# Latent stage of a small language-model tower: feed-forward up products split 128 + 64 instead of 96 + 96 rows

## The chip, the cores and the metric

One Trainium2 chip, one of its cores, one launch. The metric is the device time of the launch in microseconds. TensorE (PE, with its weight loads shown as PEld), VectorE (DVE), ScalarE (ACT), GpSimd (POOL) and SyncE (SP) each run their own instruction stream and meet at semaphores.

## The reference, cut to what matters

A tower of token embedding, quantised attention, a routed attention, a latent linear-attention block, and a mixture of eight experts, over 32 sequences of 128 tokens with 192 features. The change is in the feed-forward half of the latent block (`_L1_attn_ref`):

```
x = x + attn_out
xn = rmsnorm(x, ffn_ln_w)
ffn_out = jax.nn.silu(xn @ w1) * (xn @ w2) @ w3      # w1, w2: 192 x 512, w3: 512 x 192
return x + ffn_out
```

`xn @ w1` and `xn @ w2` contract over 192 features.

## The kernel before

The stages of the tower run one after the other. The latent stage takes 256 tokens (two tiles of 128) at a time. Two streams `p0` and `p1` alternate, each with four PSUM banks and its own buffers. `in_turns_apart` writes the order out by hand: while one stream does its first part (`..._l_1`: norms, latent attention), the other does its second part (`..._l_2`: projection, residual, feed-forward). A generator's `yield` hands over to the other stream. So one half-iteration is one first part interleaved with one second part, there are 16 pairs of tiles in all, and a loop iteration (`Fori`) holds two half-iterations, with a short DVE step (`chain_over`, L1001) after the second.

Every engine runs its instructions in the order of its program, so that order matters:

- PE in a half-iteration: the latent products of the first part (L951, L958, L1534, L1537); the transposes of the feed-forward input by `turn` (L932, called at L1563); the feed-forward up products by `product` (L958, called at L1566 and L1567, 16 matmuls, which the profile shows as 32 instructions, two to a float32 product); the transposes of the head slots (L1545); the decayed products `products` (L1505, twice 12 matmuls); the feed-forward down product (L1572); `times_v` (L1515); `turned_back` (L1523); `turn` of the attention output.
- ACT: takes the turned feed-forward input (`take_turned`, L943); gates of the first part (L1602 to L1604, L1607 to L1611); exponentials (L1615); the four Silu of the feed-forward (L1641); copies of the slots (L1620).
- DVE: the rotary work (L1401 to L1406), the gates (L1409 to L1417), the head norm (L1422, which waits for POOL), L1424, the padded slots (L1434), then the product of Silu and the second up product (L1478), then L1444.
- POOL: a power over 24 columns for each tile (L1490, twice 4.2 us), and the small powers (L998).

`turn` transposes the 192 features as two chunks of 96: four transposes, output on 96 partitions. `product` adds two matmuls of 96 rows into one bank region. Bank `c` holds columns `c` of both up products, w1's in its first half and w2's in its second, and after both the semaphore `hid_p` is raised, once for each `c`. All weights of this stage and of the one before it are loaded by one SP list (`loads_f + loads_l`) as soon as the attention is done with their place (`s_att`), and the stage before the latent one waits for all of them (`s_wf`).

Of the kernel before, what the change touches and what calls it, by code (L numbers as in the profile page):

```python
# [11 lines left out]
ACT = mybir.ActivationFunctionType  # L12
# [82 lines left out]
def tower(nc, a, out):  # L95

    with ExitStack() as ctx:
# [89 lines left out]
        def halves(name):  # L187
            return AP[name].rearrange("(c p) n -> p c n", c=2)
# [551 lines left out]
        def chunks2(x):  # L740
            return x.rearrange("p (c n) -> p c n", c=2)
# [8 lines left out]
        lw_comp, lw_cat, lw_proj = chunks2(W.take(2 * LAT)), W.take(3 * D + 4 * H + D), chunks2(W.take(2 * D))  # L750
        lw_1, lw_2 = chunks2(W.take(2 * HID)), chunks2(W.take(2 * HID))
        lw_3 = W.take(4 * D).rearrange("p (f n) -> p f n", f=4)
# [30 lines left out]
        def halves_of(name):  # L783
            return AP[name].rearrange("(c p) -> p c", c=2)
# [19 lines left out]
            (lw_cat[:, 3 * D:3 * D + 4 * H], AP["L1_attn_w_reso"]), (lw_cat[:, 3 * D + 4 * H:], AP["L1_attn_w_outgate"]),  # L804
            (lw_proj[0:C], halves("L1_attn_w_proj")), (lw_1[0:C], halves("L1_attn_w1")), (lw_2[0:C], halves("L1_attn_w2")),
            (lw_3, AP["L1_attn_w3"].rearrange("(f p) n -> p f n", f=4)),
            (l_lnw[0:C, :], halves_of("L1_attn_ln_w")), (l_fnw[0:C, :], halves_of("L1_attn_ffn_ln_w")),
            (l_memn[0:C, :], halves_of("L1_attn_memn_w")), (l_hd, rows("L1_attn_head_decay")), (l_temp, rows("L1_attn_temperature")),
            (l_qkn[:, 0:DH], rows("L1_attn_qn_w")), (l_qkn[:, DH:2 * DH], rows("L1_attn_kn_w")),
            (l_rot, AP["rotary"]), (l_cnt, AP["count"]), (l_tri, AP["causal_t"]),  # L810
        ]
        loads_m = [
            (mw_v[0:C], halves("L1_ffn_in_proj_w")[:, :, 2 * D:3 * D]), (mw_o[0:C], halves("L1_ffn_out_proj_w")),
# [122 lines left out]
        def take_turned(a, b, dst, ready, scale=None, bias=None):  # L936

            if scale is None:
                nc.scalar.activation(dst[0:C], chunks2(a.bank[b][0:C, :]), ACT.Copy).then_inc(ready, 1)  # L939
                return  # L940
            for c in range(2):
                kw = {} if bias is None else {"bias": bias[0:C, c:c + 1]}
                ins = nc.scalar.activation(dst[0:C, c, :], a.bank[b][0:C, c * NM:(c + 1) * NM], ACT.Identity,  # L943
                                           scale=scale[0:C, c:c + 1], **kw)
            ins.then_inc(ready, 1)

# [572 lines left out]
        def turned_back(pe, g, a, f, i):  # L1519
# [4 lines left out]
            mm.then_inc(f.out_p, 1)  # L1524

        def tensor_l_1(pe, g, a, f):
            pe.wait_ge(f.xr, per(g, 1, 1))
# [30 lines left out]
        def tensor_l_2(pe, g, a, f):  # L1558
# [3 lines left out]
            pe.wait_ge(f.ffn_in, per(g, 1, 1))  # L1562
            turn(a, a.xr, 2, f.xT_p)  # L1563
            pe.wait_ge(f.xT, per(g, 3, 3))
            for c in range(4):
                product(a, lw_1, slice(c * P, (c + 1) * P), a.bank[c][:, 0:NM])  # L1566
                product(a, lw_2, slice(c * P, (c + 1) * P), a.bank[c][:, NM:2 * NM]).then_inc(f.hid_p, 1)  # L1567
            yield
# [63 lines left out]
        def scalar_l_2(act, g, a, f):  # L1632
            act.wait_ge(f.x, per(g, 1, 1))
            squares(a, a.x, f.squared)
            yield
            act.wait_ge(f.xT_p, per(g, 3, 3))
            take_turned(a, 2, a.xT, f.xT, scale=l_fnw)
            yield
            for c in range(4):
                act.wait_ge(f.hid_p, per(g, 4, c + 1))  # L1640
                nc.scalar.activation(a.sil[:, c, :], a.bank[c][:, 0:NM], ACT.Silu).then_inc(f.silu, 1)  # L1641
# [699 lines left out]
```

## Time and profile before

| | |
|---|---|
| runs | 2418.88, 2419.63, 2421.25 us, median 2419.63 |
| the profiled execution, its own time | 2421.41 us |
| its span | 2419.7 us |
| busy in the span: PE, DVE, ACT, POOL | 69%, 56%, 42%, 21% |
| mean granted TensorE clock | 0.77 of full |

The span is the time from the first to the last instruction; 1.7 us of the profiled execution lie around it. TensorE's granted clock is 1.0 (2.4 GHz) or 0.5 (1.2 GHz); the page's line PEclk gives its mean in tenths for each of 40 slices. The latent stage fills about 918 to 1506 us of the span.

### The profile page before, as it was taken

The page shows a single profiled execution, that of the slowest core. Times are in us where ns is not written, and L with a number is a line of the kernel's source. Part 1 is how long each engine was busy: PE and PEld are TensorE (multiplying, and loading weights), DVE is VectorE, ACT ScalarE, POOL GpSimd, SP SyncE. Part 2 cuts the span into 40 slices and gives each one's busy share as a digit, 9 for nine tenths or more (in the row PEclk, how much of TensorE's full clock was granted, in tenths as well). Part 3 has the DMA queues.
Part 4 walks back from the last instruction along what each step waited for, and adds up shares of the span by engine and source line. Part 5 has one row for each costly group of instructions (what it writes and reads, how often), then busy time and mean ns, then how long its engine had stood idle before and what let it go on. Part 6 is the DMA issues. An engine that isn't in the chain of part 4 may idle for free.

```text
span 2419.7 us, 36535 instructions
## 1 busy us (share of the span) xinstructions
PE 1671.7 (69%) x11952; PEld 1259.0 (52%) x11952; DVE 1349.1 (56%) x4440; ACT 1008.5 (42%) x2807; POOL 496.9 (21%) x376
## 2 busy tenths in 40 slices
PE   0056555476667645777877776688788775999996
PEld 0022111364556534565665665566666663777775
DVE  2967888677677755566555553455555553121221
ACT  0244888673333333445445442233333332444342
POOL 5200111000000003233223221022222222333332
PEclk9975555555787765888888888677877877999998
DMA  3000000002993000000000000000000004777775
GB/s 75 0 0 0 1 0 0 1 0 51 188 191 58 0 1 1 1 0 0 0 0 0 0 0 1 1 21 20 20 20 20 20 20 123 183 177 179 182 176 135
DMA packets 135695, 112.72 MB, mean 47 GB/s; under 512 B 29256, under 2 KB 127784, under 8 KB 135592
## 3 DMA queue, kind: packets, MB, share of 16 engines
q1 hardware_dynamic: 118776, 91.70, 16.1%
q0 software_dynamic: 16864, 20.33, 4.5%
q8 instruction: 29, 0.48, 0.1%
q14 instruction: 26, 0.21, 0.0%
HBM read 69.19 MB, written 45.94 MB: 48 GB/s over the span
## 4 chain that ended last, share of the span: by engine, by line
PE 38%; DVE 21%; issue 18%; ACT 12%; POOL 9%; DVEq 1%; DMA 1%; SPq 0%; POOLq 0%; ACTq 0%
PE bank L2157 6%; PE bank L958 5%; ACT bank L686 5%; PE bank L2142 4%; POOL WK L1490 4%; PE bank L2146 3%; PE bank L1848 2%; POOL WK L998 2%; PE bank L1572 2%; PE bank L951 2%; PE bank L1135 2%; PE bank L932 1%; ACT WK L703 1%; PE bank L536 1%; POOL resid L2286 1%
## 5 line engine op out<-in xcount | busy, mean ns | idle before, releaser
L958 PE MATMUL bank<-WK,R 96*128 96x256 f32 x1088 | 308.2, 444 | 26.6 <-ACT WK L943 15.6
L998 POOL TENSOR_TENSOR WK<-WK,mhalf 128x2 f32<-128x2 f32 (+1 forms) x96 | 81.7, 851 | 1008.3 <-DVE WK L975 585.7
L958 PEld LDWEIGHTS bank<-WK,R 96*128 96x128 f32 x1088 | 237.9, 224 | 75.7 <-ACT WK L943 21.5
L686 ACT ACTIVATE bank<-bank,nbias,sc 128x128 f32<-128x128 f32 x384 | 168.0, 469 | 59.5 <-DVE nbias L379 59.5
L2194 ACT ACTIVATE R<-bank,WK 128x256 f32<-128x256 f32 x234 | 98.2, 471 | 218.2 <-PE bank L2146 218.2
L2049 DVE SCALAR_TENSOR_TENSOR WK<-bank,R,WK 128x192 f32<-128x192 f32 x78 | 29.0, 414 | 266.2 <-PE bank L2157 266.2
L2078 POOL DMA_INDIRECT moe_sum<-WK x78 | 121.5, 1557 | 264.1 <-DVE WK L2049 183.4
L2157 PE MATMUL bank<-R 128*128 128x192 f32 x936 | 169.2, 331 | 0.0
L932 PE MATMUL bank<-ident,WK 128*96 128x128 f32 x384 | 73.6, 324 | 126.0 <-DVE WK L981 82.7
L2157 PEld LDWEIGHTS bank<-R 128*128 128x128 f32 x936 | 150.2, 190 | 13.2 <-issue 13.2
L1490 POOL TENSOR_TENSOR WK<-WK,mhalf 128x24 f32<-128x24 f32 x32 | 133.6, 4190 | 26.1 <-DVE WK L1394 26.1
L583 PE MATMUL bank<-WK 32*128 32x128 bf16 x384 | 58.7, 300 | 108.3 <-DVE WK L372 55.6
L2142 PE MATMUL bank<-R 128*128 128x256 f32 x468 | 126.2, 393 | 1.1 <-ACT R L2185 1.1
L932 PEld LDWEIGHTS bank<-ident,WK 128*96 128x96 f32 x384 | 46.8, 147 | 153.5 <-DVE WK L981 79.8
L943 ACT ACTIVATE WK<-bank,R 96x256 f32<-96x256 f32 x128 | 58.8, 508 | 136.0 <-PE bank L932 135.9
L583 PEld LDWEIGHTS bank<-WK 32*128 32x128 bf16 x384 | 27.5, 118 | 164.7 <-ACT bank L686 102.2
L530 PE MATMUL bank<-identb,WK 128*96 128x128 bf16 x64 | 8.2, 306 | 150.2 <-DVE WK L307 137.9
L951 PE MATMUL bank<-R,WK 96*128 96x192 f32 x384 | 100.3, 419 | 14.1 <-ACT WK L939 11.6
L2142 PEld LDWEIGHTS bank<-R 128*128 128x128 f32 x468 | 84.6, 192 | 20.9 <-issue 13.2
L951 PEld LDWEIGHTS bank<-R,WK 96*128 96x128 f32 x384 | 82.1, 243 | 25.6 <-ACT WK L939 21.1
L1848 PE MATMUL bank<-WK 32*128 32x128 f32 x1536 | 83.7, 366 | 14.3 <-DVE WK L1700 4.5
L1750 DVE RECIPROCAL WK<-bank 128x12 f32<-128x12 f32 x32 | 7.4, 233 | 153.7 <-PE bank L1898 153.2
(476 smaller groups left out, 4032.6 us busy)
## 6 DMA issues: line engine op xcount, KB each, us to landing
moe_rows_in<-zeros SPq DMA_DIRECT2D x1, 25026.0 KB, 137.9
R<-in_L_ffn_w SPq DMA_DIRECT2D x39, 576.0 KB, 4.9
R<-in_L_ffn_w SPq DMA_DIRECT2D x39, 384.0 KB, 3.0
R<-moe_rows_in SPq DMA_DIRECT2D x39, 194.0 KB, 4.7
R<-in_L_ffn_w SPq DMA_DIRECT2D x78, 96.0 KB, 3.7
WK<-in_L_ffn_b SPq DMA_DIRECT2D x39, 96.0 KB, 5.5
moe_sum<-resid POOLq DMA_DIRECT2D x16, 192.0 KB, 2.4
moe_sum<-WK POOLq DMA_INDIRECT x78, 6.0
```

The costliest lines, as they stand in the source:

```text
L583: mm = nc.tensor.matmul(bank[u % 4][:, k * P:(k + 1) * P], qks[32 * j:32 * j + 32, k, i * P:(i + 1) * P], qks[32 * j:32 * j + 32, 3 + k, i ...
L686: ins = nc.scalar.activation(s, s, ACT.Exp, bias=nbias[:, u, k:k + 1], scale=col(SS), accum_out=sums[:, 3 * u + k:3 * u + k + 1])
L932: mm = nc.tensor.transpose(a.bank[b][0:C, c * NM + i * P:c * NM + (i + 1) * P], src[:, i, c * C:(c + 1) * C], ident[:, :])
L951: mm = nc.tensor.matmul(a.bank[b][:, i * D:(i + 1) * D], a.xT[0:C, c, i * P:(i + 1) * P], w[0:C, c, :], start=(c == 0), stop=(c == 1))
L958: mm = nc.tensor.matmul(out, w[0:C, c, m], a.xT[0:C, c, :], start=(c == 0), stop=(c == 1))
L998: nc.gpsimd.tensor_tensor(a.rs[:, 0:n], a.ve[:, 0:n], mhalf[:, 0:n], ALU.pow).then_inc(f.root, 1)
L1490: nc.gpsimd.tensor_tensor(a.rs[:, w], a.ve[:, w], mhalf[:, w], ALU.pow).then_inc(f.root, 1)
L1848: mm = nc.tensor.matmul(a.bank[j][:, k * P:(k + 1) * P], x, y, start=True, stop=True)
L2078: pool.indirect_dma_start(out=acc, out_offset=bass.IndirectOffsetOnAxis(ap=x_id[k % B3][:, t:t + 1].bitcast(U32), axis=0), in_=x_y[k % B3] ...
L2142: nc.tensor.matmul(bank[b + n][:, 0:NR], xw_1a[h][:, q * P:(q + 1) * P], x_T[h][:, 0, :], start=True, stop=False)
L2157: mm = nc.tensor.matmul(bank[4 + t][:, 0:D], x_hid[f][:, t * P:(t + 1) * P], xw_2[h][:, f, :], start=(p == 0 and n == 0), stop=(p == PAIRS ...
L2194: ins = nc.scalar.activation(x_hid[q], bank[(0, 2, 0)[p] + n][:, 0:NR], ACT.Gelu, bias=xb_1[h][:, q:q + 1])
```

## The change

The feature axis of the feed-forward input is split into its first 128 features and a rest of 64. `turn_doubled` transposes the first 128 and brings the rest to partitions 0 to 63 and again to 64 to 127, each by a matmul with the identity. `hidden` computes the hidden chunks in pairs: for each of w1 and w2 two matmuls over 128 rows, then two over 64 rows, the first with rows 0 to 63 into one bank, the second with rows 64 to 127 into the other. The rest rows of the weights are loaded so that the odd chunks lie on the upper partitions. `hid_p` is raised once for each pair of chunks.

```
-        lw_1, lw_2 = chunks2(W.take(2 * HID)), chunks2(W.take(2 * HID))
+        lw_1a, lw_2a, lw_1b, lw_2b = W.take(HID), W.take(HID), W.take(HID // 2), W.take(HID // 2)
...
-            (lw_proj[0:C], halves("L1_attn_w_proj")), (lw_1[0:C], halves("L1_attn_w1")), (lw_2[0:C], halves("L1_attn_w2")),
+            (lw_proj[0:C], halves("L1_attn_w_proj")), (lw_1a, AP["L1_attn_w1"][0:P, :]), (lw_2a, AP["L1_attn_w2"][0:P, :]),
...
-            (l_lnw[0:C, :], halves_of("L1_attn_ln_w")), (l_fnw[0:C, :], halves_of("L1_attn_ffn_ln_w")),
+            (l_lnw[0:C, :], halves_of("L1_attn_ln_w")), (l_fnw[:, 0:1], column("L1_attn_ffn_ln_w", 0, P)),
+            (l_fnw[0:HE, 1:2], column("L1_attn_ffn_ln_w", P, HE)), (l_fnw[HE:P, 1:2], column("L1_attn_ffn_ln_w", P, HE)),
...
+        for dst, name in ((lw_1b, "L1_attn_w1"), (lw_2b, "L1_attn_w2")):
+            for n in range(2):
+                loads_l.append((dst[HE * n:HE * (n + 1), :].rearrange("p (f n) -> p f n", f=2),
+                                AP[name][P:D, :].rearrange("p (f two n) -> p f two n", two=2, n=P)[:, :, n, :]))
...
+        def turn_doubled(a, src, b, ready):
+
+            for i in range(M):
+                w = slice(NM + i * P, NM + (i + 1) * P)
+                nc.tensor.transpose(a.bank[b][:, i * P:(i + 1) * P], src[:, i, 0:P], ident[:, :])
+                for n in range(2):
+                    mm = nc.tensor.matmul(a.bank[b][HE * n:HE * (n + 1), w], src[:, i, P:D], ident[:, :], start=True, stop=True)
+            mm.then_inc(ready, 1)
+
+        def take_doubled(a, b, dst, ready, scale):
+
+            for c in range(2):
+                ins = nc.scalar.activation(dst[:, c, :], a.bank[b][:, c * NM:(c + 1) * NM], ACT.Identity, scale=scale[:, c:c + 1])
             ins.then_inc(ready, 1)
...
+        def hidden(a, f, p):
+
+            for wa, wb, out in ((lw_1a, lw_1b, slice(0, NM)), (lw_2a, lw_2b, slice(NM, 2 * NM))):
+                for n in range(2):
+                    c = 2 * p + n
+                    nc.tensor.matmul(a.bank[c][:, out], wa[:, c * P:(c + 1) * P], a.xT[:, 0, :], start=True, stop=False)
+                for n in range(2):
+                    s = slice(HE * n, HE * (n + 1))
+                    mm = nc.tensor.matmul(a.bank[2 * p + n][:, out], wb[s, p * P:(p + 1) * P], a.xT[s, 1, :], start=False,
+                                          stop=True)
+            mm.then_inc(f.hid_p, 1)
...
-            turn(a, a.xr, 2, f.xT_p)
+            turn_doubled(a, a.xr, 2, f.xT_p)
             pe.wait_ge(f.xT, per(g, 3, 3))
-            for c in range(4):
-                product(a, lw_1, slice(c * P, (c + 1) * P), a.bank[c][:, 0:NM])
-                product(a, lw_2, slice(c * P, (c + 1) * P), a.bank[c][:, NM:2 * NM]).then_inc(f.hid_p, 1)
+            hidden(a, f, 0)
+            hidden(a, f, 1)
...
-            take_turned(a, 2, a.xT, f.xT, scale=l_fnw)
+            take_doubled(a, 2, a.xT, f.xT, l_fnw)
...
-                act.wait_ge(f.hid_p, per(g, 4, c + 1))
+                act.wait_ge(f.hid_p, per(g, 2, c // 2 + 1))
```

## Rows read from the trace of the kernel before

**Rows 1.** The page: the span, and the granted clock in 40 slices, in tenths.

```profile
span 2419.7 us, 36535 instructions
...
PEclk9975555555787765888888888677877877999998
```

**Rows 2.** Timeline of POOL, its power L1490: start, us, operation, idle before.

```profile
959.90 8.62 POOL L1490 TENSOR_TENSOR WK<-WK,mhalf 128x24 f32<-128x24 f32 x2 [1.76 <-DVE WK L1394]
...
1171.88 8.31 POOL L1490 TENSOR_TENSOR WK<-WK,mhalf 128x24 f32<-128x24 f32 x2 [1.76 <-DVE WK L1394]
1206.21 8.35 POOL L1490 TENSOR_TENSOR WK<-WK,mhalf 128x24 f32<-128x24 f32 x2 [0.70 <-DVE WK L1394]
1243.46 8.31 POOL L1490 TENSOR_TENSOR WK<-WK,mhalf 128x24 f32<-128x24 f32 x2 [1.76 <-DVE WK L1394]
...
1421.18 8.36 POOL L1490 TENSOR_TENSOR WK<-WK,mhalf 128x24 f32<-128x24 f32 x2 [0.70 <-DVE WK L1394]
```

**Rows 3.** Timeline of a half-iteration whose turn falls at the full clock.

```profile
1206.64 0.64 PE L932 MATMUL bank<-ident,WK 128*96 128x128 f32 x4 [0.29 <-DVE WK L1472]
1208.20 7.17 PE L958 MATMUL bank<-WK,R 96*128 96x256 f32 x32 [0.92 <-ACT WK L943]
1214.60 0.56 DVE L1422 TENSOR_TENSOR WK<-WK 128x384 f32<-128x384 f32 x1 [2.47 <-POOL WK L1490]
1216.97 1.53 PE L1545 MATMUL bank<-ident,WK 128*128 128x128 f32 x12 [1.59 <-DVE WK L1434]
1217.42 1.21 ACT L1641 ACTIVATE R<-bank 128x256 f32<-128x256 f32 x4
```

**Rows 4.** Timeline of the next half-iteration, whose turn falls at the half clock.

```profile
1245.55 0.88 PE L932 MATMUL bank<-ident,WK 128*96 128x128 f32 x4
1247.35 7.17 PE L958 MATMUL bank<-WK,R 96*128 96x256 f32 x32 [0.92 <-ACT WK L943]
1248.46 0.20 DVE L1409 TENSOR_TENSOR R<-R 128x24 f32<-128x24 f32 x1 [1.87 <-ACT R L1604]
1252.79 0.52 ACT L1615 ACTIVATE R<-R 128x384 f32<-128x384 f32 x1 [0.35 <-DVE R L1424]
1254.36 1.48 PE L1545 MATMUL bank<-ident,R 128*128 128x128 f32 x12
```

**Rows 5.** Timeline of PE in the expert stage, a 128 + 64 split already there.

```profile
2204.55 0.70 PE L2146 MATMUL bank<-R 64*128 64x256 f32 x4
2205.18 1.13 PE L2142 MATMUL bank<-R 128*128 128x256 f32 x4
2206.24 0.70 PE L2146 MATMUL bank<-R 64*128 64x256 f32 x4
```

**Rows 6.** Timeline of PE: matmuls of 64 output columns, and L1505 before L1572.

```profile
800.39 0.44 PE L1171 MATMUL bank<-WK 128*64 128x128 f32 x4 [0.25 <-ACT WK L1215]
...
1188.87 1.66 PE L1505 MATMUL bank<-R 32*128 32x128 f32 x24 [2.08 <-DVE R L1444]
1190.47 5.04 PE L1572 MATMUL bank<-R,WK 128*128 128x192 f32 x16
```

**Rows 7.** A window (busy by engine; then clock, DMA share, GB/s), and PE's L951.

```profile
1235.90:1246.10 10.20, 9.73 (x21) 5.66 (x20) 6.02 (x19) 5.54 (x13) 3.40 (x2) 0.50 0.00 0
...
1200.43 1.57 PE L951 MATMUL bank<-R,WK 96*128 96x192 f32 x8
1235.26 2.38 PE L951 MATMUL bank<-R,WK 96*128 96x192 f32 x8
```

**Rows 8.** Timeline at the stage's end; a window of L958 there (PE, PEld, clock).

```profile
1492.06 10.44 PE L958 MATMUL bank<-WK,R 96*128 96x256 f32 x32 [0.92 <-ACT WK L943]
...
1492.00:1503.00 11.00, 10.44 (x32) 8.32 (x32) 0.70 0.00 0
```

**Rows 9.** Timeline of SP's queue: last weight load, first issue after the attention.

```profile
588.91 0.43 SPq L775 DMA_DIRECT2D R<-in_causal_t  x1
606.01 0.65 SPq L838 DMA_DIRECT2D moe_rows_in<-zeros  x1
```

More of the change, by code:

```diff
@@ L944, in take_turned @@
                                            scale=scale[0:C, c:c + 1], **kw)
+            ins.then_inc(ready, 1)
+        def turn_doubled(a, src, b, ready):
[8 more added lines that the diff above has]
+                ins = nc.scalar.activation(dst[:, c, :], a.bank[b][:, c * NM:(c + 1) * NM], ACT.Identity, scale=scale[:, c:c + 1])
             ins.then_inc(ready, 1)
```

## The prediction

> **What bounds the kernel now.** I read the page first: the span is 2419.7 us, and in the ten slices of the latent stage (the 16th to the 25th) the clock line reads 5 once and then 8 [rows 1]: TensorE ran a good part of the time at 1.2 GHz. Then POOL's timeline gives the beat of the stage: L1490 comes once in a half-iteration, 16 times in all, and from 959.90 to 1421.18 us there are 13 intervals, 35.5 us each. From the middle of the stage on they are of two lengths in turn, 34.3 us (1171.88 to 1206.21) and 37.3 us (1206.21 to 1243.46), and a start after the long one has 1.76 us of idle time before it where the other has 0.70. Six of the 16 starts have it [rows 2].
>
> Next I followed one half-iteration to see what ends last. PE's up products, L958 x32, run from 1208.20 to 1215.37 us. At that time POOL works on L1490 until 14.6, and DVE's L1422 has waited 2.47 us for it. PE is then idle 1.59 us until L1434 lets it start L1545, and ACT's first Silu, the only reader of the up products, comes at 1217.42, 2.05 us after they are done [rows 3]. So the products that the change rewrites are not on the path of this half-iteration: POOL's power, then DVE, then ACT are. In the half-iteration after it the transposes fall at the half clock (the window 1235.9 to 1246.1 has clock 0.50 [rows 7]). They start late, behind L1537, ACT and then DVE's L1409 wait for them (1.87 us), and the exponential of the second tile sits idle only 0.35 us for its own input. PE starts L1545 right behind L958 [rows 4]. There the cover is thin.
>
> **The change part by part.** *The up products.* 32 instructions at 7.17 us are 0.22 us each, with the tail of the last. Afterwards 16 have 128 rows and 16 have 64, and two of these run side by side. The expert stage has this pattern at the same 256 columns: from one rest group at 2204.55 to the next at 2206.24, four wide and four narrow instructions, takes 1.69 us. Four wide ones alone would be 4 x 0.22 = 0.86 and two slots of rests 0.43, so 0.40 us are lost at the two changes of shape, 0.20 at each [rows 5]. `hidden` has four such groups: 4 x 1.69 = 6.76 us plus the last instruction's tail of some 0.3, against 7.17. The gain is about 0.1 us where 12 slots for 16 would promise 1.8. If the rests did not overlap at all it would be 8 x 0.20 + 32 x 0.22 = 8.6 us, 1.5 more than now; the row speaks against that.
>
> The Trainium skill, TensorEngine Tiling (Array Packing), gives up to 2x for a dimension of at most 64 under Theoretical Speedup, and says under Key Properties that a change of tiling mode drains TensorE. By the first alone the phase would be 24 x 0.22 = 5.2 us. The trace shows both, and the second takes nearly all of the first back: 6.8 us [rows 5].
>
> *The transposes.* Four at 0.64 us with their tail [rows 3] become two transposes and four matmuls of 64 columns, in pairs on separate column halves. Such matmuls are in the trace: four instructions (two float32 products) in 0.44 us, so two slots of 0.11 and the tail [rows 6]. That gives 2 x 0.11 + 4 x 0.11 = 0.65 us of slots against 0.43, plus three changes of shape (transpose to halves, back, and again) at 0.20: 0.8 us more at the full clock. Bounds: 0.2 us if this change of shape costs nothing, and 1.35 at the half clock. There the price of a change is 0.3: L1505 begins 1.60 us before L1572 with six slots of 0.21 (twice the 0.11 of the full clock), 1.28 [rows 6]; so two transposes and four slots of 0.21 and three changes are 2.2 us against 0.85. In the half-iteration of [rows 4] the clock comes back at 1246.1 [rows 7], 0.6 us after the transposes start, so I take 0.83 there.
>
> *What the delay hits.* PE has the up products behind it, ACT has L1602 to L1604, and DVE waits for these at L1409. At the full clock all of it is covered: the chain that is late by 0.8 us ends in L1422 and L1424 of the first tile, well ahead of the 2.47 us wait for POOL; the up products end at 1208.20 + 0.83 + 6.76 + 0.3 = 1216.1, before L1545 (1216.97) and Silu (1217.42) [rows 3]. Cost 0. If that cover were gone, 0.8 us for each. At the half clock the first exponential slips 0.83 us and the second has 0.35 of room, so the path grows by 0.48 us; the up products would end at 1255.2 and L1545 start 0.7 later, but ACT's table load and Silu, themselves 0.48 later, hide that [rows 4]. Six half-iterations of 16 are so [rows 2]: 6 x 0.48 = 2.9 us. Bounds: 0 (the slack holds) and 16 x 0.83 = 13 us.
>
> *The pairwise semaphore.* Silu of chunk 0 now waits for pair 0, done 3.4 us into the phase; in the loop Silu starts far later [rows 3]. Only at the stage's end nothing runs beside the phase. L958 takes 10.44 us there, at a mean clock of 0.70 over the 11 us [rows 8], so low for the first 6.6. Transposes wholly at the half clock: 1.35 later. The four groups: at the half clock 6 slots of 0.43 and 0.6 for changes are 3.2 us, 1.65 of them in the 5.2 us that are left low, then 2.35 x 1.69 = 4.0; so the products end 1502.9 against 1502.5, and one Silu of 0.38 us more stands behind the last pair: 0.8 us, once.
>
> *Loads.* 18 latent loads become 24. At some 0.47 us an issue, SP ends at 591.8 instead of 589; landings take a few us more, and the next thing that could need them starts at 606 [rows 9]. Cost 0; with no cover it would be 3 us. `take_doubled` reads 128 partitions for 96 with the same 256 columns: 0.
>
> Sum: 2.9 + 0.8 = 3.7 us on the profiled execution's 2421.41, 2425.1. The median of the runs is 1.8 lower, so **2423.3 us**, 0.15% slower.
>
> **The rivals.** *More low stretches.* The clock falls in the gap between L1515 and L951 of one half-iteration in two. Where it stays up L951 starts at 1200.43 and takes 1.57 us; where it falls L951 takes 2.38 and the half-iteration is 3 us longer [rows 2, 7]. PE does the same work before both, and the gap differs by little (the loop's turn). A path that is 0.5 us later can tip the other half-iteration over too. If all the 8 or so short ones become long: 8 x 3.0 = 24, with the 3.7 above 2447 us; if a part of them does, about 2432. For it: the two lengths keep their order over the stage, which looks like work in step with the clock's changes, and so near an edge. Against: the same coupling can swallow 0.5 us.
>
> *Fewer low stretches.* The same edge from the other side, and my case of the other sign: the clock stays up through that gap in the loop's second half-iteration, since the work lies otherwise to the clock's changes. Each long half-iteration that turns short gives back 3.0 us; two of them outweigh the 3.7 us, and with three the gain can be measured. Three to six give 9 to 18 us: 2405 to 2414 us. For it: 0.5 us is as large as the differences on which the fall hangs. Against: PE's work there comes no earlier.
>
> *It does less than it says and costs nothing.* The coupling with the clock, or more slack than I count, takes the delay of the turn: only the end's 0.8 us remain, 2420.4. A variant is that the changes of shape are cheap and the phase does shrink by up to 1.8 us; since it is covered [rows 3], the time stays the same too.
>
> *The rests do not overlap.* 8.6 us: then even the full-clock half-iterations end at 1217.9, 0.9 after L1545's start [rows 3], and the others are 1.5 to 2 later: 9 x 0.7 + 6 x 1.8 + 3 = 20 us, 2440. Rows 5 speak against it.
>
> **How the numbers follow.** Chances: my sum, or less of it where the delay is taken in (2418 to 2427), 0.55; more low stretches 0.24; fewer 0.17; no overlap 0.04. A measurement here tells 0.2%, 4.8 us, from no change: 2414.8 to 2424.5. The first case lies mostly within it (0.42) and partly above (0.13); the second and fourth are slower, 0.28 less 0.01; of the third 0.15 are faster and the rest within. So faster 0.15, same 0.45, slower 0.40. The range is 2411 to 2442: it leaves out the worst of the second rival and the best of the third.
>
> **What would show it.** Groups of `hidden` (wide and rest) at 1.69 us; the doubled turn at some 1.5 us against 0.64; DVE's L1422 still waiting for POOL, PE idle before L1545 about 0.9 us at the full clock; the spacing of L1490 in its two lengths, 34.3 and 37.3 to 37.8. Wrong: groups of 1.3 us (no price of changing), or another mix of the two lengths: that alone moves the time by more than all my terms.

## The result, and the profile after

| | before | after |
|---|---|---|
| median of nine runs each | 2420.1 us | 2425.04 us |
| lowest to highest | 2415.76 to 2421.25 | 2422.74 to 2428.25 |
| the profiled execution, its own time | 2421.41 | 2422.74 |
| its span | 2419.7 | 2421.0 |

The ratio is 1.0023, with a 95% interval of 1.0013 to 1.0033: slower by 4.9 us, just outside what a measurement here tells from no change. The forecast was 2423.3 us in a range of 2411 to 2442, with "same" a little likelier than "slower".

One thing has to be seen before the traces are compared. The profiled execution of after is the lowest of its nine, and that of before the highest of its nine. So the two traces differ by 1.3 us where the medians differ by 4.9. They show the mechanisms, but their spans don't measure the loss.

From the page of after, the span and the granted clock in 40 slices:

```profile
span 2421.0 us, 36733 instructions
...
PEclk9986555555787867888789888777778776999998
```

The timeline of PE, of the half-iteration whose turn falls at the full clock (columns as in [rows 3]):

```profile
1208.42 0.33 PE L956 MATMUL bank<-ident,WK 128*128 128x128 f32 x1 [0.28 <-DVE WK L1492]
1208.68 0.44 PE L958 MATMUL bank<-ident,WK 128*64 128x128 f32 x4
1209.05 0.33 PE L956 MATMUL bank<-ident,WK 128*128 128x128 f32 x1
1209.31 0.44 PE L958 MATMUL bank<-ident,WK 128*64 128x128 f32 x4
1210.69 1.13 PE L1551 MATMUL bank<-WK,R 128*128 128x256 f32 x4 [0.94 <-ACT WK L964]
1211.75 0.70 PE L1554 MATMUL bank<-WK,R 64*128 64x256 f32 x4
1212.38 1.13 PE L1551 MATMUL bank<-WK,R 128*128 128x256 f32 x4
...
1216.83 0.70 PE L1554 MATMUL bank<-WK,R 64*128 64x256 f32 x4
1219.34 2.30 PE L1577 MATMUL bank<-ident,WK 128*128 128x128 f32 x12 [1.81 <-DVE WK L1454]
```

The turn takes from 1208.42 to 1209.75: 1.33 us against 0.64 in [rows 3]. A group of `hidden`, two wide products and two rests, repeats after 1.69 us (1210.69 to 1212.38), and the phase ends at 1217.53, 6.84 us after its start. Before it was 7.17. PE is idle 1.81 us afterwards, where it was idle 1.59 in [rows 3]. The power's start to the slots (L1577) takes 0.6 us more than before, and that is where the idle time comes from: the forecast was some 0.9. So the up products are covered in full, as forecast.

What was not forecast is in POOL. Its timeline, the power over 24 columns (L1490 before, L1510 now):

```profile
1174.31 8.31 POOL L1510 TENSOR_TENSOR WK<-WK,mhalf 128x24 f32<-128x24 f32 x2 [1.76 <-DVE WK L1414]
1207.99 8.95 POOL L1510 TENSOR_TENSOR WK<-WK,mhalf 128x24 f32<-128x24 f32 x2 [0.70 <-DVE WK L1414]
1246.00 8.31 POOL L1510 TENSOR_TENSOR WK<-WK,mhalf 128x24 f32<-128x24 f32 x2 [1.76 <-DVE WK L1414]
...
1350.76 8.95 POOL L1510 TENSOR_TENSOR WK<-WK,mhalf 128x24 f32<-128x24 f32 x2 [0.70 <-DVE WK L1414]
1387.43 9.03 POOL L1510 TENSOR_TENSOR WK<-WK,mhalf 128x24 f32<-128x24 f32 x2 [1.03 <-DVE WK L1414]
1422.42 8.95 POOL L1510 TENSOR_TENSOR WK<-WK,mhalf 128x24 f32<-128x24 f32 x2 [0.70 <-DVE WK L1414]
```

The two powers of a half-iteration took 8.3 us in nearly all rows of before [rows 2]; now 11 of 16 rows have 8.9 to 9.0. The reason stands in DVE's timeline of the same half-iteration, first of after, then the same addition in before:

```profile
1211.75 0.20 DVE L1429 TENSOR_TENSOR R<-R 128x24 f32<-128x24 f32 x1 [0.71 <-ACT WK L1635]
...
1211.96 0.96 DVE L1431 TENSOR_TENSOR WK<-WK 128x768 f32<-128x768 f32 x1
...
1216.97 0.56 DVE L1442 TENSOR_TENSOR WK<-WK 128x384 f32<-128x384 f32 x1 [2.47 <-POOL WK L1510]
```

```profile
1209.60 0.95 DVE L1411 TENSOR_TENSOR WK<-WK 128x768 f32<-128x768 f32 x1
```

Read it so. The later turn makes ACT later, ACT the gates, and DVE now waits 0.71 us for them at L1429. Behind that wait stands a long addition of two SBUF tiles, L1431. In before it ran from 1209.60 to 1210.55, 3.39 us after the start of POOL's first power (1206.21), and the second power begins some 4.15 us after the first: 0.2 us of the addition lay past that start. In after the addition starts 3.97 us behind the first power (1207.99) and lies across the start of the second, until 1212.92. The second power then takes 4.81 us instead of 4.22. DVE's L1442 waits for it, and that wait is on the path. All traces give one relation: where the addition starts ahead of the second power, the power takes 4.02 us plus the time that the addition runs past the power's start (0.20 and 4.22, 0.45 and 4.47, 0.52 and 4.54, 0.79 and 4.81, 0.86 and 4.88), and never less than 4.15. Where the addition starts inside the power, next to nothing is lost on either side (4.16 to 4.19 us). In this row of before it starts 1.1 us into the second power, which still takes 4.16 us, and the addition its 0.95:

```profile
1248.67 0.95 DVE L1411 TENSOR_TENSOR R<-R 128x768 f32<-128x768 f32 x1
```

Here the Trainium skill bears: SBUF — State Buffer, under "SBUF: two separate sides", says that DVE with two SBUF inputs and a GpSimd operation that reads SBUF hold the shared pair of ports one at a time, for whole instructions, and that the one that started second waits. The traces agree where the addition is first: the power grows by what is left of it. They don't agree where the power is first: the addition did not wait for it.

Yet the pair of half-iterations is not longer for it. Between the last rows above, 1350.76 to 1422.42 is 71.66 us; in before, 1349.50 to 1421.18 is 71.68. Windows over these two stretches, after and then before (us, busy by engine with instruction counts for PE, PEld, DVE, ACT, POOL, then the clock):

```profile
1350.76:1422.42 71.66, 54.08 (x401) 38.65 (x400) 41.80 (x126) 32.08 (x84) 22.90 (x10) 0.88 0.00 0
```

```profile
1349.50:1421.18 71.68, 56.58 (x389) 43.90 (x388) 41.90 (x126) 32.12 (x84) 21.58 (x11) 0.83 0.00 0
```

POOL is busy 1.3 us longer, and the clock is lower for a shorter time (0.88 against 0.83 in the mean). The short interval between two power starts grew from 34.4 to 35.0 us and the long one shrank from 37.3 to 36.7. Earlier in the loop of after (power starts at 1136.31, 1174.31 and 1207.99) it is the other way about: 38.0 and 33.7, again 71.7 together. The experiments show how general this is.

### The profile page after: what moved, and what is told of

The parts are those of the page before. It is cut to its first block, busy times and chain, and to the rows that moved or that the text cites. A ratio compares the mean times of both kernels' runs of the same rounds, so it can differ in the third digit from the quotient of the medians.

```text
span 2421.0 us, 36733 instructions
## 1 busy us (share of the span) xinstructions
PE 1664.3 (69%) x12048; PEld 1221.1 (50%) x12048; DVE 1347.7 (56%) x4440; ACT 1008.5 (42%) x2807; POOL 503.8 (21%) x376
## 4 chain that ended last, share of the span: by engine, by line
PE 39%; DVE 21%; issue 18%; ACT 12%; POOL 9%; DVEq 1%; DMA 0%; SPq 0%; POOLq 0%; ACTq 0%
PE bank L2188 7%; PE bank L978 5%; ACT bank L686 5%; PE bank L2173 5%; POOL WK L1510 4%; PE bank L2177 3%; PE bank L1879 2%; POOL WK L1018 2%; PE bank L971 2%; PE bank L1603 2%; PE bank L1155 2%; PE bank L937 1%; ACT WK L703 1%; POOL resid L2317 1%; PE bank L536 1%
## 5 line engine op out<-in xcount | busy, mean ns | idle before, releaser
L978 PE MATMUL bank<-WK,R 96*128 96x256 f32 x576 | 189.1, 489 | 12.5 <-ACT WK L944 11.0
L978 PEld LDWEIGHTS bank<-WK,R 96*128 96x128 f32 x576 | 140.2, 251 | 43.3 <-ACT WK L944 15.9
L1510 POOL TENSOR_TENSOR WK<-WK,mhalf 128x24 f32<-128x24 f32 x32 | 140.3, 4403 | 24.6 <-DVE WK L1414 24.6
L937 PE MATMUL bank<-ident,WK 128*96 128x128 f32 x320 | 61.4, 324 | 118.3 <-DVE WK L1001 82.1
L937 PEld LDWEIGHTS bank<-ident,WK 128*96 128x96 f32 x320 | 38.0, 145 | 134.5 <-DVE WK L1001 78.8
L686 ACT ACTIVATION_READ_ACCUMULATOR bank<-bank,nbias,sc 128x1 f32 x384 | 94.8, 247 | 0.0
```

What stands on the lines that cost most here:

```text
L686: ins = nc.scalar.activation(s, s, ACT.Exp, bias=nbias[:, u, k:k + 1], scale=col(SS), accum_out=sums[:, 3 * u + k:3 * u + k + 1])
L937: mm = nc.tensor.transpose(a.bank[b][0:C, c * NM + i * P:c * NM + (i + 1) * P], src[:, i, c * C:(c + 1) * C], ident[:, :])
L978: mm = nc.tensor.matmul(out, w[0:C, c, m], a.xT[0:C, c, :], start=(c == 0), stop=(c == 1))
L1510: nc.gpsimd.tensor_tensor(a.rs[:, w], a.ve[:, w], mhalf[:, w], ALU.pow).then_inc(f.root, 1)
```

## The experiments

Each batch has its own runs of the kernel before, on the same chip. The first four kernels ran against a before of 2420.31 us (18 runs, 2412.85 to 2424.88). One execution of each kernel was profiled, and it isn't always a typical one: in experiments 3 and 6 it is the fastest of the kernel's runs, in 4 and 5 the slowest. Times are compared by medians; traces show mechanisms.

**1. The same split, an ordinary turn.** DVE writes the rest twice, so that the turn is four equal transposes, and the products stay as changed.

```
-                for n in range(2):
-                    mm = nc.tensor.matmul(a.bank[b][HE * n:HE * (n + 1), w], src[:, i, P:D], ident[:, :], start=True, stop=True)
+                mm = nc.tensor.transpose(a.bank[b][:, w], a.sq[:, i, 0:P], ident[:, :])
...
-                ins = nc.vector.tensor_scalar(a.xr[:, i, :], a.x[:, i, :], a.rs[:, i:i + 1], None, ALU.mult)
+                nc.vector.tensor_scalar(a.xr[:, i, 0:P], a.x[:, i, 0:P], a.rs[:, i:i + 1], None, ALU.mult)
+                ins = nc.vector.tensor_scalar(a.sq[:, i, 0:P].rearrange("p (n d) -> p n d", n=2),
+                                              a.x[:, i, P:D].unsqueeze(1).to_broadcast([P, 2, HE]), a.rs[:, i:i + 1], None,
+                                              ALU.mult)
```

> The changed kernel, but its turn is four plain transposes again: VectorE writes the rest of 64 features twice side by side, so that one transpose brings it to both halves of the partitions. No change of shape in the turn; the up products stay split 128 + 64. Theory A (the turn's delay moves the gate work of VectorE, its 768-wide addition then lies across the start of POOL's second power over 24 columns, and that power takes 4.81 us where it took 4.16 to 4.22, on the path): turn 0.65 us, second power back at 4.2 us in nearly all half-iterations, time 2419 to 2422 us, 0.1 to 0.25% under the changed kernel; VectorE's 0.3 us more for the doubled write cost up to 2 us. Theory B (my prediction: the delay bites only where the turn falls at the half clock, through the second exponential): also about 2420 to 2422, but the powers are unchanged at 4.8. Theory C (the price of the changes of shape inside the up products, or the pairwise semaphore, makes the loss): stays at 2425.

Measured: 2424.34 us, ratio 1.0018 (1.0009 to 1.0027). No better than the change, and theory A's 4.2 us missed: 12 of 16 second powers are again longer, at 4.53 to 4.57 us. That DVE's extra work is the delay here is only argued. It doesn't separate the theories.

**2. The delay alone.** The kernel before with six needless transposes ahead of its turn, and none of the split.

```
+            for n in range(6):
+                nc.tensor.transpose(a.bank[2][0:C, 0:P], a.xr[:, 0, 0:C], ident[:, :])
             turn(a, a.xr, 2, f.xT_p)
```

> The kernel before, with six more transposes ahead of the turn of the feed-forward input (the first chunk again, into the place that the turn then writes): PE's turn is 0.65 us later at the full clock, 1.3 at the half clock, nothing else changes. Theory A: second power 4.8 us in the half-iterations at the full clock, time 2424 to 2427 us, as the changed kernel. Theory B: 2422 to 2425 with powers at 4.2. Theory C: 2420, as before.

Measured: 2427.59 us, ratio 1.0029 (1.0018 to 1.0041), and 14 of 16 second powers at 4.73 to 4.81 us. A delay of the turn brings a loss (7.3 us, above the 4 to 7 expected) and the longer powers by itself, without the split.

**3. The addition ahead of the gates.** The changed kernel; DVE does L1431 before it waits for the gates.

```
+            nc.vector.tensor_tensor(a.qk, a.a, a.b, ALU.add)
             v.wait_ge(f.gates, per(g, 1, 1))
...
-            nc.vector.tensor_scalar(a.pz, a.sg[:, :, :, 2], 1.0, None, ALU.add)
-            ch.step(nc.vector.tensor_tensor(a.qk, a.a, a.b, ALU.add))
+            ch.step(nc.vector.tensor_scalar(a.pz, a.sg[:, :, :, 2], 1.0, None, ALU.add))
```

> The changed kernel, with VectorE's 768-wide addition of the rotary parts moved ahead of its wait for the gates (it needs none of them). Theory A: the addition ends before POOL's second power starts, or is over early in it; second power at 4.16 to 4.3 us, and 7 us of the stage come back: 2416 to 2420. Theory B: the gate chain is 0.95 us shorter where the turn falls at the half clock, which gives 6 x 0.48 = 3 us back: 2422, with no change of the powers. Theory C: 2425.

POOL's timeline in the half-iteration that answers to the one above:

```profile
1207.28 8.29 POOL L1510 TENSOR_TENSOR WK<-WK,mhalf 128x24 f32<-128x24 f32 x2 [0.70 <-DVE WK L1414]
```

All powers are back at 4.2 us, with the turn still late. That shows that L1431 makes the powers longer: moving one DVE instruction removes it. The same edit also takes the addition out of the chain of the gates, so what it does to the time can't be put down to the powers alone. From its first to its last row L1510 spans 530.1 us against 533.75 in after. But the time is 2432.68 us (2423.17 to 2437.88), ratio 1.0049 (1.0032 to 1.0067): the expectation of the total missed, and by its sign. Windows over the stage that follows, expert attention and routing, in after and then in this kernel:

```profile
1520.30:2032.50 512.20, 383.89 (x3524) 312.31 (x3524) 271.06 (x1076) 166.02 (x386) 110.08 (x129) 0.74 0.07 22
```

```profile
1516.00:2033.30 517.30, 384.92 (x3524) 313.51 (x3525) 271.47 (x1076) 165.96 (x386) 109.90 (x129) 0.74 0.07 22
```

The latent stage was left 4.3 us earlier, and a stage whose program is the same took 5.1 us longer. This is the fastest of the six executions, as long as the profiled one of after (2423.17 and 2422.74). Where the median loses its further 9.5 us is in no trace.

**4. The rests one after the other.** Both rests of a pair use the lower 64 rows, so the odd chunks are computed with the rest weights of the even ones.

```
-                    mm = nc.tensor.matmul(a.bank[2 * p + n][:, out], wb[s, p * P:(p + 1) * P], a.xT[s, 1, :], start=False,
+                    mm = nc.tensor.matmul(a.bank[2 * p + n][:, out], wb[0:HE, p * P:(p + 1) * P], a.xT[0:HE, 1, :], start=False,
```

> The changed kernel with both rests of a pair on the lower 64 rows (rows 0 to 63 of the turned input and of the rest weights for both banks, so the odd chunks use the even chunks' rest weights): they can't run side by side. A group of four wide and four narrow instructions should take 4 x 0.22 + 4 x 0.22 + 0.4 = 2.1 us instead of 1.69, the phase 8.6 instead of 6.9. If the up products are covered with 0.9 us to spare at the full clock: L1577 starts about 0.7 us later in each half-iteration and 10 to 20 us are lost, 2435 to 2445. If the products were on the path already (theory C): 16 x 1.7 = 27 us, 2452. If ACT's own work covers all: 2425 to 2428.

PE's timeline, two groups at the full clock, then the slots behind the last group:

```profile
1215.68 1.13 PE L1551 MATMUL bank<-WK,R 128*128 128x256 f32 x4 [0.94 <-ACT WK L964]
1216.74 1.13 PE L1553 MATMUL bank<-WK,R 64*128 64x256 f32 x4
1217.80 1.13 PE L1551 MATMUL bank<-WK,R 128*128 128x256 f32 x4
...
1224.33 1.53 PE L1576 MATMUL bank<-ident,WK 128*128 128x128 f32 x12
```

A group takes 2.12 us and the phase 8.5, so in the change the rests do overlap, and that is worth 1.7 us a phase. Here PE starts the slots without idle time: the cover is gone. The kernel takes 2433.21 us, ratio 1.0051 (1.0036 to 1.0065), a little under the 2435 to 2445 that was expected with this cover gone. And still its loop is not slower than a merely delayed one: from POOL's first row to its last it takes 537.33 us, and the kernel of experiment 2 takes 537.30. One pair of half-iterations:

```profile
1212.99:1284.66 71.67, 57.48 (x401) 41.60 (x400) 41.83 (x126) 32.11 (x84) 22.88 (x10) 0.88 0.00 0
```

Again 71.67 us. Between the profiles of after and of this kernel (spans 14.7 us apart) 8.4 us of the difference lie behind the last power's start (63.2 and 71.6 us to the next stage), at the end of the stage, where nothing runs beside the phase and it ran wholly at the half clock (1500.10 to 1516.2).

The next four ran on another chip, against a before of 2451.83 us (35 runs, 2441.34 to 2460.41), 32 us above the one of the first batch. All four profiles have the stage behind the latent one at 536 to 550 us, where the first chip had 512 to 517.

**5. No doubling by PE.** The rest of one chunk is features 0 to 63 and that of the other 128 to 191: four plain transposes of features 0 to 127 and 64 to 191, the weights loaded to match.

```
-                for n in range(2):
-                    mm = nc.tensor.matmul(a.bank[b][HE * n:HE * (n + 1), w], src[:, i, P:D], ident[:, :], start=True, stop=True)
+                mm = nc.tensor.transpose(a.bank[b][:, w], src[:, i, HE:D], ident[:, :])
...
-                    nc.tensor.matmul(a.bank[c][:, out], wa[:, c * P:(c + 1) * P], a.xT[:, 0, :], start=True, stop=False)
+                    nc.tensor.matmul(a.bank[c][:, out], wa[:, c * P:(c + 1) * P], a.xT[:, 1 - n, :], start=True, stop=False)
```

> The changed kernel with a turn that needs no doubling: four plain transposes of 128 columns, features 0 to 127 and features 64 to 191. Even chunks contract features 64 to 191 over 128 rows and features 0 to 63 in the lower row group, odd chunks features 0 to 127 and 128 to 191 in the upper one; the weights are loaded to suit. So the turn costs what it did before the change (0.64 us), VectorE does nothing extra, and the up products keep the split, its changes of shape and the pairwise semaphore. Theory A (the delayed turn makes the loss, by POOL's power and by the second exponential): POOL's second power 4.16 to 4.22 us, latent stage as before, time 2418 to 2422. Theory C (split products or semaphore make it): 2424 to 2426 still. If the free-running coupling with the clock makes any edit of the stage cost some us: anything from 2416 to 2428 with short powers.

Measured: 2458.77 us, ratio 1.0018 (1.0004 to 1.0032). Powers at 4.16 to 4.23 us: without the longer turn the addition doesn't lengthen them. But the loss did not go away. So the longer powers aren't needed for a loss, theory A missed, and theory C (the split products or the pairwise semaphore cost in the stage) stands here.

**6. The addition ahead of the gates, in the kernel before.** The edit of experiment 3 on before.

> The kernel before, with VectorE's 768-wide addition ahead of its wait for the gates, and nothing else. The powers go from 4.22 to 4.16 us, and where the turn falls at the half clock the gates are 0.95 us less late, 0.35 of which is on the path (half-iterations of 37.3 become about 36.9): latent stage 2 to 3 us shorter. Theory D (what the latent stage gives is passed on or lost by the next stage, whose time hangs on how it falls against the clock's changes, as 512 against 517 us with the same program in the changed kernel and in the one with the moved addition): the total can be 2416 or 2425, and the difference to the latent stage's own is in the next stage.

Measured: 2451.24 us, ratio 0.9996 (0.998 to 1.0013): the same. Its latent stage took 613.3 us in the profile, which is the fastest of its 12 runs: 10 less than that of before in the first batch, where 2 to 3 were expected, and the stage behind it 540.1.

**7. Experiment 3, started later.** Two needless memsets of 0.70 us ahead of the expert attention, to move that stage against the clock's changes.

```
+            for n in range(2):
+                ch.step(nc.vector.memset(streams[0].m_va, 0.0))
```

> The kernel with the moved addition (2423 to 2438 us in its runs), with VectorE clearing one buffer twice more, 1.4 us, before it releases the attention of the expert block; no other difference. Theory D (the next stage's time hangs on where it starts against the clock's changes): the next stage is no longer at 517 us, and the runs move by more than the 1.4 us put in, most likely down, to 2418 to 2428. If it does not hang on it: the stage stays at 517 and the runs are 1.4 us above, 2425 to 2439 with the same spread.

Measured: 2442.22 us (2430.17 to 2452.94), ratio 0.9964 (0.9942 to 0.9985). It does more work than before and is the only kernel that is faster. Windows over the stage behind, in experiment 6 and in this one:

```profile
1509.20:2049.30 540.10, 393.01 (x3524) 322.18 (x3525) 272.96 (x1076) 165.95 (x386) 109.88 (x129) 0.71 0.07 21
```

```profile
1523.40:2059.20 535.80, 389.04 (x3524) 319.66 (x3524) 273.15 (x1076) 166.23 (x386) 110.12 (x129) 0.72 0.07 21
```

The same instructions, 4.3 us apart, with the clock lower for longer in the longer one. In experiment 5 the same stage took 549.6 us at 0.70. So that stage's time moves by several us with its program untouched, and gains or losses of a few us in the latent stage may come back out of it with either sign. That its start sets it, as theory D has it, is not shown: it starts at 1522.3 in experiment 5 and at 1523.4 here, and takes 549.6 and 535.8 us. Nor do these two profiles explain the medians: the profiled execution of experiment 7 is 9.2 us longer than that of experiment 6 (2449.27 and 2440.08), while its median is 9.0 shorter.

**8. Fewer changes of shape.** Experiment 5 with the up products in two groups: for each weight four wide chunks, then four rests.

```
+                for c in range(4):
+                    nc.tensor.matmul(a.bank[c][:, out], wa[:, c * P:(c + 1) * P], a.xT[:, 1 - c % 2, :], start=True, stop=False)
+                for c in range(4):
+                    n, p = c % 2, c // 2
...
```

> The kernel with the overlapped turn, and the up products in two groups instead of four: all four chunks of w1 over 128 rows, their four rests, then the same for w2; hid_p is raised behind each pair of w2's rests. Four changes of shape instead of eight: 16 x 0.22 + 8 x 0.22 + 4 x 0.20 = 6.0 us with no tail, where the changed kernel has 6.76. Since the phase is covered in the loop (theory of the cover): no difference to the overlapped turn beyond 1 us, though PE is busy 12 us less. If the products were on the path: 10 us less than the overlapped turn.

```profile
1210.00 1.99 PE L1553 MATMUL bank<-WK,R 128*128 128x256 f32 x8 [0.93 <-ACT WK L967]
1211.93 1.13 PE L1557 MATMUL bank<-WK,R 64*128 64x256 f32 x8
1212.99 1.99 PE L1553 MATMUL bank<-WK,R 128*128 128x256 f32 x8
1214.91 1.14 PE L1557 MATMUL bank<-WK,R 64*128 64x256 f32 x8
1218.76 1.60 PE L1580 MATMUL bank<-ident,WK 128*128 128x128 f32 x12 [2.71 <-DVE WK L1457]
```

A group of twice the size takes 2.99 us: 8 x 0.215 + 4 x 0.215 = 2.58, and 0.41 for two changes, again 0.20 each. The phase is 6.05 us against 6.84, and PE's idle time behind it is 2.71 against 1.91 in experiment 5: the whole gain turned into idle time. The kernel takes 2460.51 us, ratio 1.0032 (1.0015 to 1.0048), 1.7 above experiment 5 and within the noise of the two (some 3.6): the expectation held.

**9 to 12. Cut off behind the latent stage.** Since the stages behind can hide a difference of 5 us, four kernels end there: the expert attention, the routing and the experts are left out (their weights are still loaded), and the residual is stored as the output. They are the kernel before, the changed one, that of experiment 5 and that of experiment 2, five runs each. In all four:

```
-            sync_x(sp)
...
+            sp.dma_start(out.rearrange("t p d -> p t d"), tiles(resid[:, :])).then_inc(s_zero, 16)
...
-            vector_m(v, ch)
-            vector_x(v, ch)
```

> The kernel before, cut off behind the latent stage: the expert block (its attention, routing and experts) is left out, all loads stay, and the residual goes to the output. It is the base for the three cut-off kernels of this group. By the profile before, the latent stage ends at 1508 us and the store takes a few us: 1515 to 1525 us in all.

> The changed kernel, cut off in the same way. Theory A and B (the loss is made in the latent stage by the delayed turn): 3 to 5 us above the cut-off kernel before, all of the measured difference. Theory D (a good part of the difference is made by the next stage, because it starts elsewhere against the clock's changes): 0 to 2 us above. In both the second power is 4.8 us in most half-iterations.

> The kernel with the overlapped turn (four plain transposes, split up products), cut off in the same way. Theory A and B: within 1.5 us of the cut-off kernel before, with only the end of the stage different (one Silu more behind the last pair, the products there a little shorter). Theory C (the split products or the semaphore cost in the stage): 3 us or more above it.

> The kernel before with six more transposes ahead of the turn, cut off in the same way. Theory A and B: 4 to 8 us above the cut-off kernel before, like the 7 us of the whole kernel with them. Theory D: 0 to 3.

| cut off behind the latent stage | median | lowest to highest | against the first |
|---|---|---|---|
| before | 1525.73 | 1523.91 to 1526.41 | |
| after | 1530.86 | 1529.65 to 1531.67 | +5.1 |
| plain overlapped turn (5) | 1528.67 | 1525.67 to 1529.42 | +2.9 |
| before with the delay (2) | 1530.38 | 1525.25 to 1531.88 | +4.7 |

The 5.1 us agree with the 4.9 of the whole kernel: so the loss arises in or before the end of the latent stage. The delay alone gives 4.7, though one of its five runs (1525.25) lies among those of before. The split without the delay gives 2.9, between what theory A (1.5 at most) and theory C (3 or more) expected. Together that is more than the whole, so the two don't add, and neither's share in the change is shown.

By the record these four ran on the first chip again. The whole kernel before took 2455.66 us there this time (nine runs, 2451.81 to 2459.59), 35 us above the first batch. So the level of a batch isn't fixed by the chip, and medians are compared only within a batch.

The lengths of the pairs, from every second start of POOL's power (us, worked out from the POOL timelines of these traces):

```
before       69.63 69.04 70.22 71.64 71.67 71.79 71.60   sum 495.6
after        70.39 70.86 71.73 71.68 71.14 71.63 71.66   sum 499.1
overlapped   69.64 71.71 71.69 71.65 71.69 71.68 71.68   sum 499.7
delayed      69.45 71.60 71.64 71.39 71.61 71.65 71.67   sum 499.0
```

Windows over the second pair, before and then after:

```profile
994.27:1063.31 69.04, 51.93 (x388) 41.00 (x388) 41.81 (x126) 32.01 (x84) 21.58 (x10) 0.90 0.00 0
```

```profile
994.96:1065.82 70.86, 55.25 (x400) 38.62 (x400) 41.89 (x126) 32.19 (x84) 22.17 (x10) 0.86 0.00 0
```

In 9 of the 14 traces at least four of the seven pairs are 71.6 to 71.7 us long, whatever their work. The traces of before have three, experiments 3 and 6 (the moved addition) two, and experiment 1 one; others in 3 and 6 are down to 68.7. A pair at that length lengthens neither with a delay nor with the 1.7 us a phase of experiment 4. Behind the first pair, a shorter one has a higher clock (experiment 6: 70.3 us at 0.85, 69.2 at 0.90, 68.8 at 0.93).

In the cut-off traces of before and after the change costs 4.1 us in the first three pairs, gives back 0.6 in the four that follow, and costs 0.3 in the last half-iteration and 1.0 behind it (1454.64 to the end of the span, 1524.0, is 69.4 us; 1458.34 to 1528.7 is 70.4), less the 0.1 that it started earlier: together the 4.7 by which the spans differ.

How much of this is the kernel, and how much the one execution that was profiled? Split all traces in the same way (us, worked out from their POOL timelines):

| | pair 1 | pairs 2 and 3 | pairs 4 to 7 |
|---|---|---|---|
| before, whole; cut off | 72.8; 69.6 | 139.9; 139.3 | 286.4; 286.7 |
| after, whole; cut off | 70.4; 70.4 | 142.6; 142.6 | 286.1; 286.1 |
| plain overlapped turn (5), whole; cut off | 69.6; 69.6 | 143.2; 143.4 | 286.7; 286.7 |
| before with the delay (2), whole; cut off | 72.6; 69.5 | 143.3; 143.2 | 286.7; 286.3 |
| experiments 1; 4; 8 | 69.7; 72.7; 70.0 | 142.0; 143.3; 142.8 | 286.9; 286.7; 286.7 |
| addition moved in the changed kernel (3; 7) | 72.2; 72.3 | 140.1; 140.1 | 283.3; 286.6 |
| addition moved in before (6) | 69.2 | 139.5 | 281.2 |

The first pair is no measure of a kernel: in the two traces of before it differs by 3.2 us, with the clock at a mean of 0.55 and 0.66 in its first half. That is the main reason why the whole loops of before and after are equally long in the first batch (533.6 and 533.8 us). The second and third pair do tell the kernels apart. They take 139.3 to 139.9 us in before and, with the addition in its old place, 142.0 to 143.4 in every kernel with the split or the delay, with long powers or with short ones. With the addition moved they are back at 140.1, split and late turn and all; in before the same move changes nothing there (139.5). So in these pairs the loss hangs on DVE's order around the gates, and not on the longer powers alone.

## Why the prediction was right, and where it was not

The total and its sign came out: 2425.0 for 2423.3, inside the narrow case of 2418 to 2427. Of the loss, 3.7 were forecast and 4.9 measured. The terms fared differently, and that they add up to nearly the right sum is in good part luck.

*The up products: right but for the tail.* Groups at 1.69 us, the phase at 6.84 for 6.76 and a tail of 0.3, the price of a change of shape at 0.20 (again 0.20 in experiments 4 and 8). At the half clock four wide products and four serial rests take 4.01 us at the end of experiment 4's stage; eight slots of 0.43 are 3.44, which leaves 0.28 for each change, for the 0.3 taken. No gain, because covered: experiment 8 shows that 0.8 us less of PE only make 0.8 more idle time. One reading was wrong without harm: ACT's Silu is not the only reader of the up products, DVE's L1478 reads the second one behind it.

*The turn: right in size.* 1.33 us at the full clock for some 1.5, and at the half clock of the stage's end 2.1 us (1493.06 to 1495.19 in PE's timeline) for 2.2.

*"At the full clock all of it is covered", "Cost 0": the step that failed.* The chain that I followed, L1422 and L1424 of the first tile, was indeed well ahead of POOL. But I took the end of POOL's power as given. A delayed DVE instruction of two SBUF inputs made it 0.6 us later. Experiment 3 took the lengthening away by moving that one instruction; experiment 2 made it without the split. That the step failed is shown; that this is what costs the time is not: experiments 5 and 8 and the third cut-off kernel have powers of 4.2 us and a loss as well.

*"6 x 0.48 = 2.9": near in size, by another way, and so by luck.* Not six but four starts of after have the 1.76 us of idle time that marks a turn at the half clock. The interval that ends at the last three of these is 38.0 us, where it was 37.1 to 37.4: a growth of the size that I had in mind. But the interval behind it is then 33.1 to 33.7, and in the last pairs the two are 36.7 and 35.0. By my own sign (another mix of the two lengths) this part was wrong. The sum of the two stays at 71.1 to 71.7, and the loss falls into the second and third pair. My remark on the first rival, that the coupling with the clock "can swallow 0.5 us", was the better description; in experiment 4 it swallows the 1.7 us of a phase. So the 2.9 us agree with what was lost in the loop (3.5 in the cut-off kernels, 495.6 to 499.1, of which 0.8 lie in the unsteady first pair) without being its working. The rival "more low stretches" has a part in it: the early pairs have a lower mean clock in after (0.86 against 0.90 above).

*The end of the stage: 0.8 forecast, not seen.* PE in after, the turn and the products with nothing beside them:

```profile
1493.06 0.48 PE L956 MATMUL bank<-ident,WK 128*128 128x128 f32 x1 [3.98 <-DVE WK L1492]
...
1496.13 2.07 PE L1551 MATMUL bank<-WK,R 128*128 128x256 f32 x4 [0.94 <-ACT WK L964]
1498.13 1.23 PE L1554 MATMUL bank<-WK,R 64*128 64x256 f32 x4
1499.29 1.38 PE L1551 MATMUL bank<-WK,R 128*128 128x256 f32 x4
1500.60 0.70 PE L1554 MATMUL bank<-WK,R 64*128 64x256 f32 x4
...
1505.96 2.88 PE L1603 MATMUL bank<-R 128*128 128x192 f32 x16 [1.27 <-DVE R L1498]
```

From the turn to the down product it is 12.90 us. In before it was 13.38, from the turn at 1490.05 to this row:

```profile
1503.43 2.88 PE L1572 MATMUL bank<-R 128*128 128x192 f32 x16 [0.93 <-DVE R L1478]
```

So this part is 0.5 us shorter: the turn starts 3.0 us later than in before, the clock comes back only 1.2 us later, and less of the phase lies at the half clock. Yet the end as a whole, from the last power's start to the next stage, is 1.0 us longer (63.2 against 62.2). The half-iteration ahead of the turn lost it: from the last power's start to this turn it is 35.97 us against 34.44, 0.7 of it in the power itself (9.01 against 8.29).

*The loads: right in their cost of 0.* The last four latent loads are issued from 590.78 on and SP is done at 593.3, for 591.8 forecast; what could need them starts at 606.

*What stays open.* The cause of the 4.9 us is not settled. A delayed turn alone makes such a loss and so does the split with a plain turn. Why the latter, with powers of 4.2 us and a shorter phase, still loses 2.9 us (its trace reaches 71.7 us two pairs earlier than before does) is not shown: the changes of shape and the pairwise semaphore were never tried apart. Its lowest run, 1525.67, lies among those of before, so part of it may be which of the early pairs happen to be short. It is also the profiled one: its loop is 4.3 us longer than that of the cut-off before, and starts 4.3 us earlier (920.31 and 924.64), so its trace shows no loss in the whole. Nor is it shown what fixes 71.67 us: the clock is down for a part of each such pair, and pairs of different work have the same length, which looks like a loop held in step with the clock's changes; no run here set out to vary that length. Why the same program took 2420 us in one batch and 2452 and 2456 in two others is open too, and the chip doesn't settle it, since the first and the last ran on the same one. Experiment 7 is no version to ship for its 0.4%: it was measured in that batch alone, and the shift that went with it was a trial.

## What to carry to other kernels

Ask of the engine that ends a wait not only when it starts but what runs beside it: a delay on one engine's chain can push a DVE operation of two SBUF inputs across the start of a POOL instruction that the path waits for. Before halving a matmul's rows to run two side by side, pay for the changes of shape: at 256 columns two changes cost as much as the two slots that were saved in a group of six. And where the granted clock changes inside a loop, don't add up half-iterations: count how many iterations still run below the length that they tend to, or cut the kernel off behind the stage and time that. See where the profiled execution lies among the runs before a few us of its trace are explained: one pair moved by 3.2 us between two traces of the same program.

## What the runs showed of the hardware that was not expected

- A POOL power of 128x24 float32 takes 4.2 us, and 4.8 to 4.9 where a 128x768 DVE addition of two SBUF tiles (0.95 us) starts just ahead of it; 11 of 16 in the changed kernel. Over all traces it is then 4.02 us plus what is left of the addition when the power starts, and at least 4.15. Where the addition starts inside the power, the two take 4.16 to 4.19 and 0.95 us.
- A pair of half-iterations takes 71.6 to 71.7 us in kernels whose up products take 6.0, 6.8, 7.2 and 8.5 us, at mean clocks of 0.81, 0.83 and 0.88.
- A stage whose program is untouched took 511.9 to 517.3 us in the six traces of one batch and 535.8 to 549.6 in the four of another, at mean clocks from 0.75 down to 0.70. The whole kernel before took 2420 us in one batch on a chip and 2456 in another on the same chip.
